# Narrow heads as row tiles of TensorE: two heads side by side, operand rows kept by chunk of tokens

## The chip, the cores and the metric

One core of one Trainium2 chip runs the whole program. The time is device microseconds of one execution. The kernel before takes 4517.99 us, the median of three runs (4517.69 to 4519.41).

## The reference, cut to what matters

The program is a stack of residual blocks on 2048 tokens of 128 features. Four of them hold attention with 16 heads of 8 features each; one of the four is causal. Per head it computes

```python
q = (x @ Wq + bq); k = (x @ Wk + bk); v = (x @ Wv + bv)      # 2048 x 128, cut into 16 heads of 8
scores = einsum('bhqd,bhkd->bhqk', rope(q), rope(k)) / sqrt(8)
scores = where(causal, scores, -inf)                          # one of the four
out = einsum('bhqk,bhkd->bhqd', softmax(scores), v)           # heads joined: 2048 x 128
x = x + out @ Wo + bo
```

The kernel treats the 2048 tokens as one sequence. Two of the four attentions stand in gated blocks, where sigmoid scales per head replace the rotation. Everything else (convolution, experts, quantised feed-forward) is not touched by the change.

## The kernel before, in words

The program is a list of stages, each with a part for every engine. An attention is a stage `Prepare`, a stage `Heads` and a projection.

**Prepare.** The tokens are cut into 4 chunks of 512 (`NC` chunks of `CH`). For each chunk TensorE projects to q, k and v, VectorE (and GpSimd for the rotation) transforms them, TensorE turns q and k so that features lie on partitions (L1471), and ScalarE and VectorE split each float32 value into three bfloat16 parts, high, middle and low (L1499 to L1527). SyncE then stores the parts to DRAM (`parts_dram`, L1537, two DMAs of 384 KB a chunk) and gathers them back as operand rows (`gather_rows`, L1299 to L1308). A product of two numbers in three parts each has 9 terms, so a head of 8 features becomes 72 rows (`KR` = `TERMS` x `HD`), plus 3 rows for the maximum (`KM` = 75). One operand tile holds one head at partitions 0 to 74, four heads behind one another, for one group of four heads (`QP`, `KP`); two groups have room at a time. Prepare gathers group 0, chunk by chunk: 6 DMAs of 96 KB a chunk. The groups 1 to 3 are gathered by SyncE within `Heads`, 6 DMAs of 384 KB each, while earlier groups are worked on. The source of each gather has its three repeated or successive parts as the outermost dimension (L1307).

**Heads.** The work is cut into 16 units, a unit being one group of 4 heads and one chunk of 512 queries. `HeadsPlan` writes out one order of steps that every engine follows. For a unit there are two passes. The first finds the maximum of each query's scores: TensorE multiplies 128 queries with 512 keys into one bank (L1732; in the causal attention the diagonal block gets a mask added by an identity product, L1735), and VectorE reduces the bank to its maximum (L1817). There are 64 such maxima a unit (16 to 64 in the causal attention); three banks take turns, so maximum n+3 waits for the reduction of maximum n. VectorE then joins and splits the maxima (L1824 to L1835), TensorE turns them (L1740), VectorE copies them out (L1841), and SyncE sends them through DRAM (L1706, L1708) into the three extra rows of the query operand. The second pass: for each tile j of 128 keys and each of the 4 heads TensorE multiplies keys with the 512 queries (L1752, mask L1755), ScalarE takes the exponential of two banks at once (L1793; L1796 and L1797 where the widths differ), and TensorE multiplies with the values (L1767), four heads as column tiles of 32 columns of the array, float32, 8 instructions for one j. The scores take turns in two pairs of banks. After the last j ScalarE copies the result (L1804), TensorE turns it (L1776), and VectorE divides by the sums (L1850, L1852).

In the plan the maxima of the next units are laid between the scores of the current one: a clock ticks once for each pair of score products, and the maxima of a unit are spread so that they end `LEAD` = 8 ticks before its scores begin; the turn of the maxima comes 3 ticks after their last. The values of a batch of two j follow one batch later. For one j the order on TensorE is thus score, maximum, score, maximum, and so on, four of each, and then the 8 value instructions.

Of the kernel before, what the change touches and what calls it, by code (L numbers as in the profile page):

```python
# [23 lines left out]
NG = HEADS // GH  # L24
SPLIT = 3
TERMS = SPLIT * SPLIT
# [14 lines left out]
             wqkv2=3 * P, bqkv2=3 * P, wo2=P, bo2=P, cos2=NT * 16, sin2=NT * 16, iota=E,  # L41
             ka=KD, kab=KD, kc=NK)
LATE = dict(wqkv3=3 * P, bqkv3=3 * P, wo3=P, bo3=P, cos3=NT * 16, sin3=NT * 16,
# [61 lines left out]
class Chip:  # L105


    def __init__(self, ctx, nc, d, out):
# [33 lines left out]
        self.mr = sb("mr", [P, 2, 16])  # L142
        self.nmb = sb("nmb", [P, 2, 3 * 16], BF16)
# [9 lines left out]
        self.parts_dram = nc.dram_tensor("parts_dram", (2, SPLIT, NG, HD, GH * T), BF16, kind="Internal").ap()  # L153
# [1128 lines left out]
def qkv(c):  # L1282
    return c.arena[:, 16384:16384 + NT * 384].rearrange("p (i n) -> p i n", i=NT)


def rotated(c):
    return c.arena[:, 4096:4096 + NT * 256].rearrange("p (i n) -> p i n", i=NT)


def packed(c):  # L1290

    both = c.arena[:, 0:16384].bitcast(BF16).rearrange("p (w s h t) -> p w s h t", w=2, s=2, h=GH)
    return both[:, 0], both[:, 1]


GATHERS = 2 * SPLIT


def gather_rows(e, c, g, t0, n, marks):  # L1299
    QP, KP = packed(c)  # L1300
    slot = g % 2
    for a in range(SPLIT):
        rows = slice(SPLIT * HD * a, SPLIT * HD * (a + 1))
        for dst, which, first, step in ((QP, 0, a, 0), (KP, 1, 0, P * T)):
            src = bass.AP(tensor=c.parts_dram.tensor,
                          offset=(which * SPLIT + first) * P * T + g * HD * GH * T + t0,
                          ap=[[step, SPLIT], [GH * T, HD], [T, GH], [1, n]])  # L1307
            e.dma_start(dst[rows, slot, :, t0:t0 + n], src).then_inc(marks.sem, 16)  # L1308


class Rope:


    def __init__(self, chip, cos, sin):
        self.c, self.cos, self.sin = chip, cos, sin
        self.src = rotated(chip)
        self.v = chip.sig.claim("rope_vector", 3 * NC)
        self.g = chip.sig.claim("rope_gpsimd", 3 * NC)
        half = GH * HD // 2
        self.x = qkv(chip)[:, :, 0:2 * P].rearrange("p i (g a n) -> p i g a n", a=2, n=half)  # L1320
        self.r = self.src[:, :, :].rearrange("p i (g a n) -> p i g a n", a=2, n=half)
        self.tmp = [[chip.arena[:, at:at + CH].rearrange("p (i g n) -> p i g n", i=TPC, g=2 * NG)
                     for at in range(12288 + 2048 * b, 12288 + 2048 * (b + 1), CH)] for b in range(2)]

    def factors(self, k):
        half = GH * HD // 2
        span, shape = slice(TPC * k, TPC * k + TPC), (P, TPC, 2 * NG, half)
        cs = self.cos.rearrange("p (i n) -> p i n", i=NT)[:, span, :].unsqueeze(2).broadcast_to(shape)
        sn = self.sin.rearrange("p (i n) -> p i n", i=NT)[:, span, :].unsqueeze(2).broadcast_to(shape)
        return span, self.x[:, span, :, 0, :], self.x[:, span, :, 1, :], cs, sn, self.tmp[k % 2]  # L1330

    def vector(self, e, k, made):
        span, x1, x2, cs, sn, tmp = self.factors(k)
# [8 lines left out]
        e.tensor_tensor(self.r[:, span, :, 0, :], tmp[0], tmp[1], ALU.subtract).then_inc(self.v.sem, 1)  # L1342

    def gpsimd(self, e, k, made):
        span, x1, x2, cs, sn, tmp = self.factors(k)
# [8 lines left out]
        e.tensor_tensor(self.r[:, span, :, 1, :], tmp[2], tmp[3], ALU.add).then_inc(self.g.sem, 1)  # L1354
# [9 lines left out]
class Temper:  # L1364


    def __init__(self, chip, scale):
        self.c, self.scale = chip, scale
        self.src = qkv(chip)
        self.prod = chip.arena[:, 4096:4096 + NT * P].rearrange("p (i n) -> p i n", i=NT)  # L1370
        self.zs = chip.arena[:, 6144:6144 + NT * HEADS].rearrange("p (i n) -> p i n", i=NT)
        self.v = chip.sig.claim("temper_vector", 7 * NC)
        self.s = chip.sig.claim("temper_sigmoid", NC)

    def z(self, k):
        return self.zs[:, TPC * k:TPC * k + TPC, :].rearrange("p i n -> p (i n)")

    def vector(self, e, k, made):
        span, z, v = slice(TPC * k, TPC * k + TPC), self.z(k), self.v
        e.wait_ge(*made)  # L1380
        e.tensor_tensor(self.prod[:, span, :], self.src[:, span, 0:P], bc(self.scale, TPC), ALU.mult).then_inc(v.sem, 1)
        e.wait_ge(*v[7 * k])
        e.tensor_reduce(z, self.prod[:, span, :].rearrange("p i (g d h) -> p (i g) h d", g=NG, h=GH), AX,
                        ALU.add).then_inc(v.sem, 1)
        e.wait_ge(*self.s[k])
        e.tensor_scalar(z, z, 2.0, None, ALU.mult).then_inc(v.sem, 1)
        e.wait_ge(*v[7 * k + 2])
        z4 = z.rearrange("p (i g h) -> p i g h", g=NG, h=GH)
        for g in range(NG):
            q4 = self.src[:, span, 32 * g:32 * g + 32].rearrange("p i (d h) -> p i d h", h=GH)  # L1390
            e.tensor_tensor(q4, q4, z4[:, :, g, :].unsqueeze(2).broadcast_to((P, TPC, HD, GH)),
                            ALU.mult).then_inc(v.sem, 1)

    def scalar(self, e, k):
        z = self.z(k)
        e.wait_ge(*self.v[7 * k + 1])
# [5 lines left out]
    def ready(self, e, k):  # L1402
        e.wait_ge(*self.v[7 * k + 6])


class Prepare(Stage):


    def __init__(self, chip, before, weights, bias, transform):
# [4 lines left out]
        self.ones = sig.claim("rows_of_ones", 2)  # L1414
# [10 lines left out]
        self.gathered = sig.dma("gather0", GATHERS * NC)  # L1425
        self.rem = chip.arena[:, 22528:22528 + 2 * CH].rearrange("p (a n) -> p a n", a=2)
# [999 lines left out]
```

## Time and profile before

| what | us |
|---|---|
| median of three runs | 4517.99 |
| the profiled execution, its own time | 4526.3 |
| span of that execution | 4524.5 |
| TensorE busy in it | 3962.3 |
| VectorE busy | 3194.4 |
| ScalarE busy | 2199.4 |

Two spans of time matter in the pages behind this table: an instruction's own duration, and the distance from its start to the start of the next one on its engine, which is shorter, since instructions overlap. In the profile the clock granted to TensorE is 1.00 at full speed (2.4 GHz) and 0.50 at half (1.2 GHz).

### The profile page before, as it was taken

The page shows a single profiled execution, that of the slowest core. Times are in us where ns is not written, and L with a number is a line of the kernel's source. Part 1 is how long each engine was busy: PE and PEld are TensorE (multiplying, and loading weights), DVE is VectorE, ACT ScalarE, POOL GpSimd, SP SyncE. Part 2 cuts the span into 40 slices and gives each one's busy share as a digit, 9 for nine tenths or more (in the row PEclk, how much of TensorE's full clock was granted, in tenths as well). Part 3 has the DMA queues.
Part 4 walks back from the last instruction along what each step waited for, and adds up shares of the span by engine and source line. Part 5 has one row for each costly group of instructions (what it writes and reads, how often), then busy time and mean ns, then how long its engine had stood idle before and what let it go on. Part 6 is the DMA issues. An engine that isn't in the chain of part 4 may idle for free.

```text
span 4524.5 us, 59451 instructions
## 1 busy us (share of the span) xinstructions
PE 3962.3 (88%) x22108; PEld 1619.8 (36%) x22108; DVE 3194.4 (71%) x6776; ACT 2199.4 (49%) x2694; POOL 97.5 (2%) x59
## 2 busy tenths in 40 slices
PE   5989797599999984999999986399894899999986
PEld 3756655122222232222222363133232232222253
DVE  5256255688888835888888548486774888888546
ACT  2222321166666651466666721156473266666721
POOL 0000000200000001000000001100001000000000
PEclk8889898599999995799999988599897699999988
DMA  0011500100000002000000000100001000000000
GB/s 23 4 43 25 116 1 6 70 1 22 2 22 2 2 6 77 12 2 22 22 2 1 20 1 0 70 2 23 22 2 47 24 2 22 11 13 2 1 19 10
DMA packets 37282, 87.42 MB, mean 19 GB/s; under 512 B 7080, under 2 KB 31432, under 8 KB 32200
## 3 DMA queue, kind: packets, MB, share of 16 engines
q1 hardware_dynamic: 36856, 82.09, 5.7%
q8 instruction: 182, 2.98, 0.3%
q10 hardware_dynamic: 144, 1.53, 0.1%
q14 instruction: 100, 0.82, 0.1%
HBM read 68.91 MB, written 14.70 MB: 18 GB/s over the span
## 4 chain that ended last, share of the span: by engine, by line
PE 75%; DVE 16%; DMA 3%; ACT 2%; SPq 2%; issue 2%; POOL 0%; ACTq 0%; DVEq 0%
PE ps L1767 18%; PE ps L1752 18%; PE ps L1732 15%; DVE pm L1817 8%; PE ps L945 3%; PE ps L948 3%; PE ps L2058 3%; PE ps L1024 3%; PE ps L2034 3%; SPq L1308 2%; DMA m_dram<-mt 1%; PE ps L1458 1%; DVE XN L289 1%; PE ps L1208 1%; PE ps L744 1%
## 5 line engine op out<-in xcount | busy, mean ns | idle before, releaser
L1817 DVE TENSOR_REDUCE pm<-ps 128x1 f32<-128x512 f32 (+2 forms) x3712 | 2258.9, 669 | 453.6 <-PE ps L1732 413.8
L1793 ACT ACTIVATE arena<-ps 128x1024 f32<-128x1024 f32 x1728 | 1684.8, 1022 | 791.5 <-PE ps L1752 788.1
L1732 PE MATMUL ps<-arena 72*128 72x512 bf16 (+2 forms) x3712 | 1453.5, 398 | 154.3 <-DMA arena<-parts_dram 127.6
L1752 PE MATMUL ps<-arena 75*128 75x512 bf16 (+1 forms) x3712 | 1385.7, 382 | 57.1 <-DMA arena<-m_dram 52.1
L1767 PE MATMUL ps<-arena,VA 128*16 128x512 f32 (+2 forms) x7424 | 965.7, 592 | 0.0
L1752 PEld LDWEIGHTS ps<-arena 75*128 75x128 bf16 x3712 | 357.1, 98 | 1098.6 <-issue 771.5
L1732 PEld LDWEIGHTS ps<-arena 72*128 72x128 bf16 x3712 | 368.6, 100 | 672.9 <-DVE pm L1817 338.0
L1767 PEld LDWEIGHTS ps<-arena,VA 128*16 128x16 f32 x7424 | 122.9, 94 | 310.8 <-issue 299.8
L976 DVE TENSOR_TENSOR arena<-EV,ps 128x512 f32<-128x512 f32 x128 | 87.8, 686 | 125.4 <-PE ps L948 120.8
L964 ACT ACTIVATE EV<-ps 128x512 f32<-128x512 f32 x128 | 76.2, 597 | 203.5 <-PE ps L945 203.5
L945 PE MATMUL ps<-XNT,arena 128*128 128x512 f32 x304 | 160.9, 612 | 2.3 <-DVE arena L1251 1.5
L948 PE MATMUL ps<-XNT,arena 128*128 128x512 f32 x304 | 158.4, 603 | 0.0
L315 PE MATMUL ps<-IDF,XN 128*128 128x128 f32 x176 | 51.2, 446 | 108.5 <-DVE XN L289 107.7
L2058 PE MATMUL ps<-arena,EV 128*128 128x512 f32 x256 | 124.1, 629 | 15.5 <-ACT EV L2246 15.5
L1850 DVE RECIPROCAL rd<-ps 128x16 f32<-128x16 f32 x64 | 15.9, 248 | 144.9 <-PE ps L1776 144.8
L1024 PEld LDWEIGHTS ps<-arena 128*128 128x128 f32 x1024 | 115.3, 192 | 2.9 <-issue 2.9
L1024 PE MATMUL ps<-arena 128*128 128x128 f32 x1024 | 115.3, 275 | 0.0
L1793 ACT ACT_TABLE_LOAD x3 | 3.8, 1283 | 225.8 <-PE ps L1752 225.8
L1078 DVE SCALAR_TENSOR_TENSOR X<-ps,prob,X 128x128 f32<-128x128 f32 x256 | 89.7, 351 | 29.1 <-PE ps L1024 22.1
L1796 ACT ACTIVATE arena<-ps 128x512 f32<-128x512 f32 (+1 forms) x128 | 63.0, 492 | 93.9 <-PE ps L1755 93.5
L1458 PE MATMUL ps<-early,XNT 128*128 128x384 f32 x128 | 66.2, 658 | 48.2 <-DVE arena L1487 26.4
L948 PEld LDWEIGHTS ps<-XNT,arena 128*128 128x128 f32 x304 | 59.2, 195 | 75.8 <-issue 74.8
(263 smaller groups left out, 2795.6 us busy)
## 6 DMA issues: line engine op xcount, KB each, us to landing
arena<-parts_dram SPq DMA_DIRECT2D x72, 384.0 KB
parts_dram<-parts SPq DMA_DIRECT2D x32, 384.0 KB, 3.4
arena<-k_dram SPq DMA_DIRECT2D x20, 528.0 KB, 11.2
arena<-parts_dram SPq DMA_DIRECT2D x96, 96.0 KB
parts<-k_dram SPq DMA_DIRECT2D x8, 528.0 KB, 6.4
arena<-in_w SPq DMA_DIRECT2D x4, 1024.0 KB, 6.2
VA<-k_dram SPq DMA_DIRECT2D x4, 528.0 KB, 7.4
arena<-in_w12T SPq DMA_DIRECT2D x1, 2048.0 KB, 13.2
```

Source lines behind the costliest of these rows:

```text
L945: e.matmul(c.bank(b), self.first(j), rhs, start=True, stop=True).then_inc(self.gate.sem, 1)
L948: e.matmul(c.bank(2 + b), self.second(j), rhs, start=True, stop=True).then_inc(self.up.sem, 1)
L1024: ins = e.matmul(c.bank(4 + g % 4)[:, q * P:(q + 1) * P], self.HT[(k - 1) % 2][:, 2 * ex + s, tt * P:(tt + 1) * P], w3[:, 2 * ex + s, :], ...
L1308: e.dma_start(dst[rows, slot, :, t0:t0 + n], src).then_inc(marks.sem, 16)
L1458: e.matmul(c.bank(2 + i % 2)[:, 0:3 * P], c.XNT[:, i * P:(i + 1) * P], self.weights, start=True, stop=True).then_inc(self.projected.sem, 1)
L1732: ins = e.matmul(bank[:, 0:w], QP[0:KR, g % 2, hh, i * P:(i + 1) * P], KP[0:KR, g % 2, hh, kc * CH:kc * CH + w], start=True, stop=not diag)
L1752: ins = e.matmul(bank[:, off:CH], KP[0:KM, g % 2, hh, j * P:(j + 1) * P], QP[0:KM, g % 2, hh, q * CH + off:(q + 1) * CH], start=True, stop ...
L1767: ins = e.matmul(c.bank(4)[32 * hh:32 * hh + VW, off:CH], c.VA[:, j, GH * g + hh, :], self.PB[:, n % self.PBS, jj, off:CH], start=j == 0, ...
L1793: e.activation(self.PB[:, pb, :, :], c.bank(2 * k, 2).rearrange("p (a t) -> p a t", a=2), ACT.Exp, scale=self.scale).then_inc(self.exped.s ...
L1817: e.tensor_reduce(c.pm[:, u % 2, hh * TPC + qt, kc:kc + 1], self.slot_bank(slot)[:, 0:w], AX, ALU.max).then_inc(self.emptied.sem, 1)
L2034: ins = e.matmul(c.bank(2 + h)[:, 0:H1], self.masks[k % 2][:, ex, at:at + P], self.w1[:, ex * H1:(ex + 1) * H1], start=False, stop=ex == E ...
L2058: ins = e.matmul(c.bank(2 + 2 * k + half), self.HTt[k][:, s * P:(s + 1) * P], self.w2[:, s, half * CH:(half + 1) * CH], start=s == 0, stop ...
```

## The change

Two heads become two row tiles of the array. The three least of the nine terms are dropped (six remain, named by `Q_PARTS` and `K_PARTS`), so a head has 48 rows and 51 with its maximum; an even head stands at partitions 0 to 50 and an odd one at 64 to 114. Products of the two heads of a pair go to different row tiles and different banks.

- **Rows by chunk.** `parts_dram` and the operands are laid out by chunk of tokens, with all 8 pairs of heads in each, so all groups are gathered in Prepare: 12 DMAs a chunk, 4 of each of three shapes (3, 2 and 1 terms outermost; 192, 128 and 64 KB). `Heads` gathers nothing and waits once, at its start, for all of them. q, k and v of a chunk are kept for two chunks only.
- **Rows of ones** come by two DMAs instead of a GpSimd memset.
- **Heads.** A maximum is one product of a 48-row tile into one bank as before, odd head first, then even; the two scores of a pair are issued back to back into two banks, and one exponential takes both. In the causal attention both halves of a pair have equal widths, so the exponential stays one instruction. The values of one j are one group of 8 instructions behind the next j's scores.
- **The maxima.** VectorE only joins them; five GpSimd instructions split them; ScalarE copies out the turned rows; two DMAs (one for each row tile) write them into the operand. `LEAD` is 9, and the turn comes 4 ticks after the last maximum.
- **Order.** For one j: a pair of scores, 2 maxima, a pair of scores, 2 maxima, the values of the j before.

```diff
-TERMS = SPLIT * SPLIT
+Q_PARTS = (0, 0, 0, 1, 1, 2)
+K_PARTS = (0, 1, 2, 0, 1, 0)
+TERMS = len(Q_PARTS)
...
-GATHERS = 2 * SPLIT
+GATHERS = 12
...
+def gather_rows(e, c, k, marks):
+    for w, rows in enumerate(packed(c)):
+        for par in range(2):
+            for term, part, step in ((0, 0, w), (3, 1 - w, w), (5, 2 * (1 - w), 0)):
+                n_terms = {0: 3, 3: 2, 5: 1}[term]
+                src = bass.AP(tensor=c.parts_dram.tensor,
+                              offset=((k * 2 + w) * SPLIT + part) * P * CH + par * (P // 2) * CH,
+                              ap=[[step * P * CH, n_terms], [PAIRS * CH, HD], [1, PAIRS * CH]])
+                first = par * (P // 2) + term * HD
+                e.dma_start(rows[first:first + n_terms * HD, k, :, :], src).then_inc(marks.sem, 16)
...
-    LEAD = 8
+    LEAD = 9
...
-        steps = [(u, hh, qt, kc) for hh in range(GH) for qt in range(TPC)
-                 for kc in range(k + 1 if self.causal else NC)]
+        steps = [(u, pp, qt, kc, par) for pp in range(2) for qt in range(TPC)
+                 for kc in range(k + 1 if self.causal else NC) for par in (1, 0)]
...
+                    self.score_pair(u, j, pp)
+                    for _ in range(n):
+                        self.run(pending.pop(0))
+                    self.tick()
+                waiting.append((u, j, first, j == n_keys - 1))
+                if len(waiting) > 1:
+                    self.values(*waiting.pop(0))
...
     def gpsimd(self, e):
+        for u in range(len(self.plan.units)):
+            k = u % 2
+            e.wait_ge(*self.top[u])
...
+            e.tensor_scalar(c.neg[:, k, :], c.mx[:, k, :], -1.0, None, ALU.mult).then_inc(s.sem, 1)
+            e.tensor_copy(c.nmb[:, k, 0:16], c.neg[:, k, :]).then_inc(s.sem, 1)
+            e.tensor_tensor(c.mr[:, k, :], c.neg[:, k, :], c.nmb[:, k, 0:16], ALU.subtract).then_inc(s.sem, 1)
+            e.tensor_copy(c.nmb[:, k, 16:32], c.mr[:, k, :]).then_inc(s.sem, 1)
+            e.tensor_tensor(c.nmb[:, k, 32:48], c.mr[:, k, :], c.nmb[:, k, 16:32], ALU.subtract).then_inc(s.sem, 1)
...
     def tensor(self, e):
+        e.wait_ge(*self.gathered)
...
+                rows = slice(64 * par, 64 * par + KR)
+                ins = e.matmul(bank[:, 0:w], QR[rows, q, 2 * g + pp, qt * P:(qt + 1) * P],
+                               KT[rows, kc, 2 * g + pp, 0:w], start=True, stop=not diag)
...
+                for par in range(2):
+                    rows = slice(64 * par, 64 * par + KM)
+                    ins = e.matmul(c.bank((t + par) % 4)[:, off:CH], KT[rows, j // TPC, 2 * g + pp, j % TPC * P:(j % TPC + 1) * P],
+                                   QR[rows, q, 2 * g + pp, off:CH], start=True, stop=not diag)
```

## Rows read from the trace of the kernel before

**Rows 1.** The page's header, and chain shares by engine (its part 4).
```profile
span 4524.5 us, 59451 instructions
PE 75%; DVE 16%; DMA 3%; ACT 2%; SPq 2%; issue 2%; POOL 0%; ACTq 0%; DVEq 0%
```
**Rows 2.** Windows: stretch, length, busy time and instructions per engine, clock, DMA share, GB/s.
```profile
770.00:855.80 85.80, 28.27 (x81) 16.90 (x80) 44.45 (x94) 16.02 (x29) 33.35 (x19) 0.64 0.19 65
900.40:1600.00 699.60, 693.84 (x3862) 207.04 (x3863) 617.13 (x1078) 471.61 (x490) 0.00 (x0) 0.99 0.02 8
990.80:1037.27 46.47, 46.13 (x262) 13.85 (x261) 41.13 (x73) 31.73 (x33) 0.00 (x0) 1.00 0.01 2
```
**Rows 3.** Timeline of one j in a plain attention: start, length, engine, line.
```profile
1000.65 0.38 PE L1752 MATMUL ps<-arena 75*128 75x512 bf16 x1
...
1000.87 0.38 PE L1732 MATMUL ps<-arena 72*128 72x512 bf16 x1
...
1001.18 1.05 PE L1767 MATMUL ps<-arena,VA 128*16 128x512 f32 x8
1002.16 0.39 PE L1752 MATMUL ps<-arena 75*128 75x512 bf16 x1
...
1002.39 0.38 PE L1732 MATMUL ps<-arena 72*128 72x512 bf16 x1
...
1002.81 2.48 DVE L1817 TENSOR_REDUCE pm<-ps 128x1 f32<-128x512 f32 x4 [0.35 <-PE ps L1732]
...
1003.02 1.94 ACT L1793 ACTIVATE arena<-ps 128x1024 f32<-128x1024 f32 x2 [0.89 <-PE ps L1752]
...
1003.48 0.38 PE L1752 MATMUL ps<-arena 75*128 75x512 bf16 x1
```
**Rows 4.** Groups by form: busy us, mean ns, idle before.
```profile
L1817 DVE TENSOR_REDUCE pm<-ps 128x1 f32<-128x512 f32 x3520 | 2195.9, 682 | 415.6 <-PE ps L1732 413.8 <-PE ps L1735 1.1
L1735 PE MATMUL ps<-MQB,IDB 128*128 128x128 bf16 x256 | 60.4, 237 | 0.0
L1446 POOL TENSOR_TENSOR parts<-arena,parts 128x512 bf16<-128x512 f32 x16 | 18.5, 1154 | 107.4 <-ACT parts L1527 107.4
L2419 POOL MEMSET const-bfloat16-1.0<- 128x1 bf16 x1 | 0.1, 113 | 0.0
```
**Rows 5.** Timeline: a maximum waits for its bank.
```profile
1551.90 2.47 DVE L1817 TENSOR_REDUCE pm<-ps 128x1 f32<-128x512 f32 x4
...
1552.63 0.10 PEld L1732 LDWEIGHTS ps<-arena 72*128 72x128 bf16 x1 [0.83 <-DVE pm L1817]
```
**Rows 6.** The chain at the start of the first Heads: start, length, what.
```profile
847.78 7.98 DMA arena<-parts_dram
...
856.52 38.36 DVE pm L1817 x64
...
896.66 1.39 DMA m_dram<-mt
898.06 2.28 DMA arena<-m_dram
```
**Rows 7.** Timeline of SyncE's queue at the end of the first Prepare.
```profile
815.38 4.64 SPq L1308 DMA_DIRECT2D arena<-parts_dram  x6
822.62 2.86 SPq L1537 DMA_DIRECT2D parts_dram<-parts  x2
825.58 5.33 SPq L1308 DMA_DIRECT2D arena<-parts_dram  x6
830.96 2.22 SPq L1537 DMA_DIRECT2D parts_dram<-parts  x2
833.29 21.04 SPq L1308 DMA_DIRECT2D arena<-parts_dram  x18
```
**Rows 8.** Windows in which only gathers move (columns as in rows 2).
```profile
848.00:852.00 4.00, 0.00 (x0) 0.00 (x0) 0.00 (x0) 0.00 (x0) 0.00 (x0) 0.50 0.20 72
2892.00:2913.00 21.00, 0.27 (x1) 0.11 (x1) 0.85 (x5) 0.00 (x0) 0.00 (x0) 0.50 0.18 78
```
**Rows 9.** DMA issues by shape: count, KB each, us from issue to landing.
```profile
parts_dram<-parts SPq DMA_DIRECT2D x32, 384.0 KB, 3.4
arena<-in_w SPq DMA_DIRECT2D x4, 1024.0 KB, 6.2
```
**Rows 10.** The two longest pieces of the chain in the causal Heads.
```profile
3173.67 26.55 DMA m_dram<-mt
2893.44 19.37 DMA m_dram<-mt
```
**Rows 11.** Windows: causal Heads; after its second wait; clock beside partly busy TensorE.
```profile
2883.50:3429.00 545.50, 486.06 (x3200) 182.66 (x3200) 380.96 (x780) 293.78 (x467) 0.38 (x1) 0.90 0.04 15
3203.00:3227.00 24.00, 24.00 (x88) 7.95 (x87) 15.39 (x32) 8.79 (x9) 0.00 (x0) 0.50 0.00 1
860.00:870.00 10.00, 10.00 (x18) 1.77 (x17) 10.00 (x18) 0.00 (x0) 0.00 (x0) 0.50 0.19 82
452.30:469.30 17.00, 12.17 (x222) 11.92 (x219) 2.44 (x2) 4.32 (x3) 0.00 (x0) 1.00 0.84 176
```

More of the change, by code:

```diff
@@ L1591, in tick, with keys, score_pair, values @@
                 self.run(item[1])
-    def batches(self, k):
-        n = TPC * (k + 1) if self.causal else NT
-        return [(j, j + 1) for j in range(0, n, 2)]
-    def offsets(self, k, pair):
-        return [max(0, (j - TPC * k) * P) if self.causal else 0 for j in pair]
-    def values(self, items, u, last):
-        for jj in range(2):
-            self.steps.append(("values", u, jj, items, last))
-            yield
+    def keys(self, k):
+        return TPC * (k + 1) if self.causal else NT
+    def score_pair(self, u, j, pp):
+        q = self.units[u][1]
+        off = max(0, (j - TPC * q) * P) if self.causal else 0
+        first = self.tiles
+        self.tiles += 2
+        self.tile_off += [off, off]
+        self.steps.append(("scores", u, j, pp, first))
+        while len(self.exp_of) < self.tiles:
+            t = len(self.exp_of)
+            n = 2
+            self.exp_of += [self.exps] * n
+            self.steps.append(("exp", t, n, self.exps))
+            self.exps += 1
+    def values(self, u, j, first, last):
+        self.steps.append(("values", u, j, first, last))
         if last:
+            self.last_tile[u] = first + 3
             self.steps.append(("empty", u))
-            self.later.append([3, ("out", u)])
+            self.later.append([4, ("out", u)])
     def lay_out(self):
         units = self.units
-        self.steps.append(("gather", 1))
         for step in self.maxima(0):
@@ L1615, in lay_out @@
         for _, k in units:
-            starts.append(starts[-1] + len(self.batches(k)) * GH)
-        pending, reached, queued, total, clock, waiting = [], 0, [], 0, 0, None
+            starts.append(starts[-1] + 2 * self.keys(k))
+        pending, reached, queued, total, clock = [], 0, [], 0, 0
+        waiting = []
         for u, (g, k) in enumerate(units):
-            if u % NC == 0 and 1 <= g < NG - 1:
-                self.steps.append(("gather", g + 1))
-            todo = self.batches(k)
-            for b, pair in enumerate(todo):
-                items = []
-                for hh in range(GH):
+            n_keys = self.keys(k)
+            for j in range(n_keys):
+                first = self.tiles
+                for pp in range(2):
                     while reached < min(u + 2, len(units) - 1):
@@ L1754, in tensor @@
                 if diag:
-                    ins = e.matmul(bank[:, off:off + P], c.IDB[:, :], c.MKB[:, :], start=False, stop=True)
-                if jj == 1:
-                    ins.then_inc(self.scored.sem, 1)
+                    for par in range(2):
+                        ins = e.matmul(c.bank((t + par) % 4)[:, off:off + P], c.IDB[:, :], c.MKB[:, :], start=False,
+                                       stop=True)
+                ins.then_inc(self.scored.sem, 1)
             elif what == "values":
-                _, u, jj, items, last = step
+                _, u, j, first, last = step
@@ L2403, in layout @@
     return {
+        "ones": np.full((1, PAIRS * T // 2), ONE_PAIR, np.float32),
         "x": i["L0_attn_input_data"].reshape(T, P),
```

353 lines of the change are left out of this document (165 added, 188 removed).

## The prediction

> **What bounds the kernel now.** I read the share of each engine in the chain first, then windows by stage, then the timeline of one step within the longest stage, and last what stands in the chain where TensorE is idle. The chain is three quarters TensorE [rows 1]. The three plain attentions make up half of the span: one takes some 740 us in `Heads`, with TensorE busy 99% of it and at the full clock [rows 2]. One unit takes 46.47 us there [rows 2], and one j 2.83 us: seven steps of 0.22 us from product to product, 0.31 from the last product to the values, and 0.98 for the values [rows 3]; 7 x 0.22 + 0.31 + 0.98 = 2.83. Sixteen of these are 45.3 us, and 1.1 us a unit is the rest (turns of maxima and results). VectorE is busy 2.48 of the 2.83 us and waits 0.35 for TensorE; ScalarE works 1.94 [rows 3]. So TensorE is the limit, VectorE not far behind: with a product always ready a reduction starts every 38.36 / 64 = 0.60 us [rows 6], four take 2.40.
>
> Between Prepare and Heads no engine works: from the first gather's issue at 815.4 to its last landing at 855.8 the gathers of the last chunks are waited for [rows 6, 7]. While they alone move, the rate is 72 to 78 GB/s at a DMA share of 0.18 to 0.20, three of sixteen engines [rows 8]; a store of 384 KB takes 3.4 us and a load of 1024 KB 6.2 us, or 165 GB/s [rows 9]. The gathers are slow by their shape, three parts outermost.
>
> **The change part by part.** The sum is made against the profiled execution, 4526.3 us (span 4524.5); that is 8 us above the median of the runs, 4518, to which I apply the differences.
>
> *Scores and maxima, plain attention.* Instructions stay as many. If both heads of a pair run side by side, a pair of scores takes 0.22 us instead of 0.44, its bounds; I take 0.22, since rows of two disjoint halves of the array have no operand in common, and keep 0.44 for a rival. TensorE's own work for a j would fall to about 2.0 us, and something else must be late next. It is not VectorE alone but the banks: three serve four maxima. A maximum whose bank is reduced from time 0 can be issued at 0.73 (1551.90 to 1552.63) [rows 5]: 0.68 of reduction [rows 4] and 0.05 for the signal. For the fourth maximum of a j that is the first one's bank. Behind it on the queue stand the values (0.31, then 0.98), then a pair of scores (0.22), then the next first maximum, whose reduction starts 0.42 after its issue (1002.39 to 1002.81) [rows 3]. The circle is 0.73 + 0.31 + 0.98 + 0.22 + 0.42 = 2.66 us a j, above VectorE's 2.40 and ScalarE's 1.94. So the gain is 0.17 us a j, 2.7 a unit. In the rest of a unit the split of the maxima leaves VectorE, but the join (0.22) and the division (0.56) fall into a circle with no slack, and a slot now waits for ScalarE behind an exponential: I take 0.4 back, so 2.3 a unit.
>
> That holds for 13 units. The first has 3 maxima a tick, 6 a j: VectorE and the banks hold it before and after alike, apart from its first 16 us at half clock, where six maxima and four scores on TensorE cost more than now; I take -4. The last two run out of maxima and are near ScalarE's pace: -2. Heads proper: -4 - 30 - 2 = -36.
>
> *The maxima's way.* At the start of a stage it is bare: 5.5 us from the last maximum to the first score [rows 6]. Four VectorE instructions go (0.85 us with their gaps), five of GpSimd come. The trace has none of their size: 0.11 us for a memset of one column is below, 1.15 for 512 columns above [rows 4]; with 16 columns I take 0.35, 1.8 in all. The second DMA adds its issue, 0.7. So +2 a stage. In steady state the turn is 4 ticks (5.3 us) after the last maximum, so TensorE, which would wait in front of all scores, doesn't: 0.25 + 1.8. From the turn to the scores are 5 ticks, 6.6 us, for 1.5 (ScalarE's queue), 1.4 (to DRAM), 0.7, 2.3 (back) = 5.9: hidden, narrowly. At 1.15 us each the split alone takes 5.8, and each unit would lose some 2 to 3 us: the upper bound.
>
> *Gathers, all of them in front.* Before, a stage gathered 24 x 96 KB = 2.36 MB before its first maximum and the other 7.1 MB behind work. After, it is 4 chunks x 4 x (192 + 128 + 64) KB = 6.29 MB, and TensorE's first maximum waits for all. At 78 GB/s [rows 8] the 3.93 MB more cost 50 us. Nothing hides them: Prepare's own work ends where it did (829), SyncE's 48 issues at 0.77 us (4.64 / 6 [rows 7]) take 37 us and are hidden under the transfers. The last gather waits for the last store, which stands behind gather 1 on its engines; gather 2 was issued before and fills that time. Bounds: spread like a plain load at 165 GB/s, 38 us in all, +7; two- and one-term gathers on only two and one engines (each a third of 78 GB/s, the first of them carrying every gather), 6.29 / 2 MB on each step of 26 GB/s, 121 us, +91. I take +50: half of the bytes have exactly the shape of the row.
>
> The Trainium skill, "DMA: Bandwidth & Descriptors", section "Why a DMA increments its semaphore by 16 and not by 1", says that the slowest dimension of both sides picks the engines: the largest number up to 16 that divides both, the lowest-numbered ones. For a 3-row source that is three engines; by that rule the trace agrees. By it the new shapes use 3, 2 and 8 engines, and the first engine carries 2.2 MB at 26 GB/s, 86 us: 6 us more a stage, a sum higher by some 24.
>
> *Plain attention, sum:* +50 + 2 - 36 = +16, three times +48.
>
> *Causal attention* (545.5 us [rows 11]). +50 and +2 again. But two pieces of its chain go: m_dram writes of 19.37 and 26.55 us that stood behind the gathers of later groups on the same engines; alone one takes 1.39 [rows 6, 10]. That is -43. After the second of them TensorE ran 24 us fully busy at a clock of 0.50 [rows 11]; without the pause I take -8. The pairs save some 59 us of products on TensorE, half on the path. Against it, 256 diagonal maxima [rows 4] and 128 diagonal pairs of scores alternate between 64-row products and a 128-row mask product, 768 changes of shape. The nearest row is the change to and from the value group, 0.31 - 0.22 = 0.09 and 0.98 less 0.85 of columns = 0.13 [rows 3]; none is below. I take 0.06, half on the path, and for both together -5. Sum: +50 + 2 - 43 - 8 - 5 = -4.
>
> The Trainium skill, "TensorEngine Tiling (Array Packing)", section "Key Properties", states that changing the tiling mode drains TensorE. The trace agrees at the values. At 0.11 for every mask change the causal stage would be some 20 us slower than in my sum.
>
> *Prepare.* The same elements in fewer or equal instructions; the memset of GpSimd was hidden; the two-chunk buffers wait for turns that were already waited for: 0.
>
> Total +48 - 4 = +44 us, 4562 on the median.
>
> **The rivals.**
> 1. *The gathers spread* over many engines. For: stores and loads do [rows 9]. Against: the outermost dimension is still 3, 2 or 1. +7 instead of +50, four times: 4390, faster.
> 2. *The circle of the banks is broken* and VectorE's 2.40 to 2.45 is reached, because half-height products deliver sooner or the values are entered without the 0.09 and 0.13. For: VectorE alone holds 0.60. Against: three banks. 0.23 x 16 x 14 x 3 = 155 less: 4407.
> 3. *Row tiles don't overlap.* Circle 2.88 instead of 2.66, above the 2.83 of now: 3.5 us a unit worse than in my sum, 150 for three stages, 35 in the causal one: 4747. No row shows two row tiles together; four column tiles do overlap at the values [rows 3].
> 4. *Gathers narrower:* +91 instead of +50: 4726.
> 5. *The clock stays at half speed.* TensorE is less filled. Through the first unit's maxima, one product in 0.60 us, the granted clock stays at 0.50; but in another stretch, busy 12.2 of 17 us, it stays at 1.00 [rows 11], and at half speed the circle keeps TensorE nearly full, as before its rise now. The circle would be 0.73 + 0.52 + 1.84 + 0.43 + 0.63 = 4.15: some 5600.
>
> **How the numbers follow.** My forecast 0.55, with its own range 4515 to 4610 (shape changes, GpSimd, rate of gathers); rivals 0.12, 0.09, 0.12, 0.08, 0.04. The range 4375 to 4730 leaves out parts of the first, third and last. A measurement can tell about 0.2%, 9 us. Faster: rivals 1 and 2 and 0.08 of my own case (steady gain over 3.5 us a unit), 0.29; within 0.2%: 0.07; slower: 0.64.
>
> **What would show it.** The first maximum of a plain stage some 90 us after the first gather's issue instead of 40, with three engines' rate in between; a j at 2.66 us with VectorE waiting 0.26 of it; two score products starting within 0.05 us; no long m_dram piece in the causal stage. Wrong if gathers move at over 100 GB/s, or if a unit takes under 42 us or over 46.

## The result, and the profile after

The changed kernel takes 4645.6 us (median of 4 runs, 4637 to 4649), the kernel before 4518.7: a ratio of 1.028, 95% interval 1.026 to 1.029. That is 127 us slower, where 44 had been forecast. The profiled execution took 4642.1 us, its span is 115.7 us longer than that of before; the other 11 us are the 8 by which the profiled execution of before lay above its median and the 3.5 by which this one lies below its own. The page of the changed kernel, as in [rows 1]:

```profile
span 4640.2 us, 57712 instructions
PE 60%; DVE 24%; DMA 4%; SPq 4%; issue 4%; ACT 3%; POOL 0%; ACTq 0%; DVEq 0%; POOLq 0%
```
The chain has lost TensorE (75 to 60%) to VectorE and to the gathers with SyncE's queue. Windows of the changed kernel (stretch, length, busy time and instructions of PE, PEld, DVE, ACT, POOL, granted clock, DMA share, GB/s): from the first gather to the first maximum, a part in which only gathers move [rows 8], the first plain Heads, a unit as in [rows 2], and the causal Heads.

```profile
818.62:912.54 93.92, 5.04 (x19) 3.21 (x17) 9.38 (x12) 5.09 (x9) 7.26 (x5) 0.50 0.24 88
855.80:905.00 49.20, 0.00 (x0) 0.00 (x0) 0.48 (x1) 0.00 (x0) 0.00 (x0) 0.50 0.19 70
912.54:1671.52 758.98, 656.98 (x4176) 149.38 (x4176) 644.19 (x1072) 507.35 (x545) 17.33 (x80) 0.95 0.01 1
1099.08:1143.50 44.42, 38.50 (x265) 9.10 (x261) 40.36 (x68) 31.66 (x34) 1.08 (x5) 1.00 0.01 1
2984.97:3519.07 534.10, 501.62 (x3152) 141.31 (x3152) 366.31 (x688) 289.66 (x353) 17.32 (x80) 0.84 0.01 2
```
The same two stages in the kernel before:

```profile
855.89:1643.93 788.04, 773.48 (x4176) 222.22 (x4176) 657.71 (x1152) 509.21 (x529) 0.00 (x0) 0.96 0.03 10
2883.53:3419.55 536.02, 479.73 (x3152) 177.16 (x3152) 373.92 (x768) 292.59 (x465) 0.00 (x0) 0.90 0.04 15
```
The stages cut at the first maximum's product and at the end of the last division give the whole difference of the spans. The forecast's "+2 a stage" for the maxima's way lies behind the first maximum, so it is counted with Heads:

| piece | forecast | measured |
|---|---|---|
| before the first maximum, four stages | +200 | 51.6 + 52.7 + 50.8 + 52.6 = +207.7 |
| Heads, three plain stages | -102 | -29.0 - 29.6 - 35.5 = -94.1 |
| Heads, causal | -54 | -1.9 |
| stages before the first Prepare, and the end | 0 | +5.1 - 0.9 |
| sum | +44 | +115.7 (rounded pieces: 115.9) |

The gathers came within 3 us a stage of the forecast. The causal Heads, which should have gained 54 us, gained 2: that is where the forecast failed. The chain from the last gather to the write of the turned maxima, as in [rows 6]:

```profile
888.84 23.56 DMA arena<-parts_dram
...
913.17 38.36 DVE pm L1864 x64
...
951.97 0.27 POOL neg L1722
...
953.14 0.23 POOL nmb L1730
...
954.25 1.40 DMA m_dram<-mt
```
One j of a plain stage, as in [rows 3]: two products of a pair start in one line of 0.39 us, and VectorE waits 0.21 us of 2.70.

```profile
1102.60 2.48 DVE L1864 TENSOR_REDUCE pm<-ps 128x1 f32<-128x512 f32 x4 [0.21 <-PE ps L1771]
...
1103.35 0.39 PE L1771 MATMUL ps<-arena 48*128 48x512 bf16 x1 [0.35 <-DVE pm L1864]
...
1103.67 1.05 PE L1807 MATMUL ps<-arena,VA 128*16 128x512 f32 x8
...
1104.65 0.39 PE L1792 MATMUL ps<-arena 51*128 51x512 bf16 x2
...
1104.88 0.38 PE L1771 MATMUL ps<-arena 48*128 48x512 bf16 x2
...
1105.30 2.48 DVE L1864 TENSOR_REDUCE pm<-ps 128x1 f32<-128x512 f32 x4 [0.21 <-PE ps L1771]
```
In the causal stage a mask (L1774) of 128 rows stands between maxima of 48 rows:

```profile
3109.71 0.38 PE L1771 MATMUL ps<-arena 48*128 48x512 bf16 x1
3110.02 0.23 PE L1774 MATMUL ps<-MQB,IDB 128*128 128x128 bf16 x1
3110.19 0.39 PE L1771 MATMUL ps<-arena 48*128 48x512 bf16 x1
```
A product of 512 columns normally lets the next start after 0.22 us; here the mask starts after 0.31. The mask has a quarter of the columns, 0.055 us, and the next product starts after 0.17. So each change of shape costs 0.09 to 0.12 us, where I had taken 0.06. For a pair of scores two masks (L1796) follow the pair, one for each bank:

```profile
3112.34 0.39 PE L1792 MATMUL ps<-arena 51*128 51x512 bf16 x2
3112.66 0.28 PE L1796 MATMUL ps<-MKB,IDB 128*128 128x128 bf16 x2
3112.88 0.39 PE L1771 MATMUL ps<-arena 48*128 48x512 bf16 x2
```
Without masks the next products would start 0.22 us behind the pair; they start 0.54 behind it, so the two masks with their changes take 0.32.

### The profile page after: what moved, and what is told of

It is laid out like the page before. It is cut to its first block, busy times and chain, and to the rows that moved or that the text cites. A ratio compares the mean times of both kernels' runs of the same rounds, so it can differ in the third digit from the quotient of the medians.

```text
span 4640.2 us, 57712 instructions
## 1 busy us (share of the span) xinstructions
PE 3634.9 (78%) x22108; PEld 1368.0 (29%) x22108; DVE 3135.8 (68%) x6440; ACT 2190.9 (47%) x2630; POOL 138.7 (3%) x371
## 4 chain that ended last, share of the span: by engine, by line
PE 60%; DVE 24%; DMA 4%; SPq 4%; issue 4%; ACT 3%; POOL 0%; ACTq 0%; DVEq 0%; POOLq 0%
PE ps L1807 18%; DVE pm L1864 17%; PE ps L1771 12%; PE ps L1792 7%; SPq L1321 4%; PE ps L949 3%; PE ps L952 3%; PE ps L2089 3%; PE ps L2065 2%; PE ps L1028 2%; DMA arena<-parts_dram 2%; ACT arena L1830 1%; PE ps L1471 1%; DMA parts_dram<-parts 1%; PE ps L1212 1%
## 5 line engine op out<-in xcount | busy, mean ns | idle before, releaser
L1830 ACT ACTIVATE arena<-ps 128x1024 f32<-128x1024 f32 (+3 forms) x1856 | 1763.9, 1000 | 827.3 <-PE ps L1792 695.0
L1771 PE MATMUL ps<-arena 48*128 48x512 bf16 (+2 forms) x3712 | 1161.8, 403 | 602.2 <-DMA arena<-parts_dram 341.9
L1807 PE MATMUL ps<-arena,VA 128*16 128x512 f32 (+2 forms) x7424 | 982.8, 602 | 2.2 <-ACT arena L1830 1.6
L1792 PE MATMUL ps<-arena 51*128 51x512 bf16 (+1 forms) x3712 | 739.6, 387 | 33.4 <-DMA arena<-m_dram 19.2
L1771 PEld LDWEIGHTS ps<-arena 48*128 48x128 bf16 x3712 | 284.2, 95 | 1246.4 <-DVE pm L1864 866.8
L1792 PEld LDWEIGHTS ps<-arena 51*128 51x128 bf16 x3712 | 185.1, 95 | 937.9 <-ACT arena L1830 670.4
L1843 ACT ACTIVATE mt<-ps 48x128 bf16<-48x128 bf16 x64 | 17.2, 270 | 469.5 <-PE ps L1779 469.5
L1807 PEld LDWEIGHTS ps<-arena,VA 128*16 128x16 f32 x7424 | 121.9, 94 | 206.1 <-ACT arena L1830 157.7
L1722 POOL TENSOR_SCALAR neg<-mx 128x16 f32<-128x16 f32 x64 | 16.2, 252 | 2907.5 <-DVE mx L1873 2907.5
```

Of the source, the lines that this page charges most:

```text
L1771: ins = e.matmul(bank[:, 0:w], QR[rows, q, 2 * g + pp, qt * P:(qt + 1) * P], KT[rows, kc, 2 * g + pp, 0:w], start=True, stop=not diag)
L1792: ins = e.matmul(c.bank((t + par) % 4)[:, off:CH], KT[rows, j // TPC, 2 * g + pp, j % TPC * P:(j % TPC + 1) * P], QR[rows, q, 2 * g + pp, ...
L1807: ins = e.matmul(c.bank(4)[32 * hh:32 * hh + VW, off:CH], c.VA[:, j, GH * g + hh, :], self.PB[:, (first + hh) % self.PBS, off:CH], start=j ...
L1830: e.activation(self.PB[:, s:s + 2, offs[0]:CH], c.bank(t % 4, 2).rearrange("p (a t) -> p a t", a=2)[:, :, offs[0]:CH], ACT.Exp, scale=self ...
```

## The experiments

Theory: in the causal stage the masks cost more by the change, at every clock, and TensorE's lower granted clock takes the rest. Rival: the masks cost before what they cost now, and clock or overlap alone explain the loss. All kernels are variants of the changed one but for e6. Ratios are to the kernel before.

**e1_spread.** Each gather cut into DMAs of one term.
```
-                src = ... ap=[[step * P * CH, n_terms], [PAIRS * CH, HD], [1, PAIRS * CH]])
+                for n in range(n_terms):
+                    src = ... ap=[[PAIRS * CH, HD], [1, PAIRS * CH]])
+                    first = par * (P // 2) + (term + n) * HD
```


> After the change, with each gather of 3 or 2 terms cut into DMAs of one term (8 partitions of 8 KB each, 24 DMAs per chunk instead of 12, same bytes). Theory 1 (the gathers are slow since an outermost dimension of 3 or 2 leaves most DMA engines idle): the stretch from the first gather to the first maximum, 93.9 us in Attention 1 of the changed kernel, falls by 38 to 48 us in each of the four stages, the median to some 4455 to 4495 us. Rival (the bytes or the count of issues on SP's queue bound them): the stretch stays within 10 us, or grows with twice the issues, the median within 4610 to 4690 us. Heads themselves keep their lengths (759, 760, 534, 759 us) but for what the clock does at their start.

4487.1 us, ratio 0.992 (0.991 to 0.994): 158 us less than the changed kernel, and faster than the kernel before. From the first gather to the first maximum's reduction, and while only gathers move:

```profile
815.79:864.06 48.27, 5.65 (x21) 3.31 (x19) 9.36 (x13) 5.09 (x9) 7.25 (x5) 0.50 0.55 171
840.00:850.00 10.00, 0.00 (x0) 0.00 (x0) 0.48 (x1) 0.00 (x0) 0.00 (x0) 0.50 0.52 188
```
94 us have become 48 in the first stage and 54, 52 and 54 in the others (to the first maximum's product), with the same bytes in twice as many DMAs; the share is 0.52 where it was 0.19. Heads kept their lengths within 2 us (757.6, 761.0, 535.0, 758.8). Theory 1 holds: the shape, not the bytes nor the number of issues, made the gathers slow. The Trainium skill, "DMA: Bandwidth & Descriptors", section "Why a DMA increments its semaphore by 16 and not by 1", lets the slowest dimension pick the engines, here 8 of 16 for every gather instead of 3, 2 and 8 by turns: by that rule the trace agrees (0.52 of 16 is 8.3).

**e2_half_masks.** The mask as two products of 64 rows and 64 columns, in the row tile of its own head.
```
-                    ins = e.matmul(bank[:, w - P:w], c.IDB[:, :], c.MQB[:, :], start=False, stop=True)
+                    half = slice(64 * par, 64 * par + 64)
+                    for h in range(2):
+                        at = w - P + 64 * h
+                        ins = e.matmul(bank[:, at:at + 64], c.MH[half, 192 - 64 * h:320 - 64 * h],
+                                       c.IDB[half, half], start=False, stop=h == 1)
```
(and the scores' masks likewise)

> After the change, with the causal mask added in the head's own row tile: two products of 64 rows and 64 columns instead of one of 128 rows and 128 columns, for the maxima and for the scores of attention 3 alone. Theory 1 (each mask product costs some 0.10 us before and 0.10 us behind it for its change of shape, 384 of them): causal Heads fall from 534 us by 30 to 60 us, median 4585 to 4615 us. Theory 2 (causal Heads are slow since TensorE's granted clock stays at half speed there, and the shapes have no share in it): Heads of attention 3 stay within 10 us of 534 and the granted clock there is as before. If the shapes also keep the clock down (their drains leave the array idle), both the length and the stretches at 0.50 shrink together. The other stages stay as they are; the early stages gain some 0.5 us from six small copies.

4598.1 us, ratio 1.017 (1.015 to 1.019), 47 less. The causal Heads fell from 534 to 489 us, the others stayed within 3 us (760.6, 757.5, 756.1): theory 1. A timeline shows the four half masks (L1807) of a pair of scores, which hold TensorE for 0.06 us where the two whole ones took 0.32:

```profile
3106.44 0.22 PE L1807 MATMUL ps<-IDB,MH 64*128 64x64 bf16 x4
3106.50 0.27 PE L1775 MATMUL ps<-arena 48*128 48x256 bf16 x2
```

**e3_maxima_first.**
```
-                    self.score_pair(u, j, pp)
                     for _ in range(n):
                         self.run(pending.pop(0))
+                    self.score_pair(u, j, pp)
```


> After the change, with the two or so maxima of each pair of scores put ahead of that pair in the order that all engines follow, nothing else. Theory 1 (steady Heads run round a circle of TensorE, ScalarE and the four score banks, 2.70 us per j, in which the maxima lie between the exponential's end and the next scores): with the maxima ahead of the wait for the banks, they leave the circle, a unit falls from 44.4 us to 39 to 42 us, plain Heads by 40 to 80 us each, median 4430 to 4540 us. Rival (VectorE's reductions bound it, or TensorE's total work): a unit stays at 44.4 us within 0.7 us, median within 4620 to 4670 us. The other side: the next pair of scores now waits behind maxima whose own banks are not yet reduced, a unit grows to 46 us or more, median above 4670 us.

4601.8 us, ratio 1.017 (1.015 to 1.019), 44 less, but not as theory 1 has it: plain Heads gained 7, 7 and 3 us (3 is what unchanged stages differ from trace to trace), the causal ones 18. One j still took 2.69 us, and now the values waited for ScalarE, behind scores that waited for the previous values:

```profile
1103.77 0.38 PE L1792 MATMUL ps<-arena 51*128 51x512 bf16 x2
...
1104.20 2.19 ACT L1830 ACTIVATE arena<-ps 128x1024 f32<-128x1024 f32 x2 [0.50 <-PE ps L1792]
...
1105.25 1.05 PE L1807 MATMUL ps<-arena,VA 128*16 128x512 f32 x8
1106.23 0.10 PEld L1771 LDWEIGHTS ps<-arena 48*128 48x128 bf16 x2 [0.85 <-DVE pm L1864]
```
**e4_warm.**
```
+        for _ in range(340):
+            e.matmul(c.bank(6), c.IDB[:, :], c.parts[:, 0, 0, 0:CH], start=True, stop=True)
         e.wait_ge(*self.gathered)
```


> After the change, with 340 more products of 128 rows and 512 columns (their result is not used) on TensorE at the start of every Heads stage, in the wait of 84 to 87 us for the gathers. Theory 1 (TensorE starts Heads at half clock and pays for it there): the granted clock is 1.00 at the first maximum, and Heads get shorter by 8 to 20 us in plain stages and 15 to 40 us in the causal one, where it stays at half clock for more than 100 us of the first 250; median 4560 to 4610 us. Rival (the clock of the causal stage follows its own sparse work, whatever it starts with): the causal stage falls back to 0.50 at the same places and Heads 3 gain under 10 us. If half speed at the start is covered by VectorE and ScalarE anyway, the median stays within 4630 to 4660 us.

4765.7 us, ratio 1.053 (1.052 to 1.055). My estimate of the wait's free part was wrong: the fence of the stage releases TensorE at 868.5, so the 75 us of products ended at 943.8, 31 us after the maxima could have begun. What it was made for it still tells. Full array at full clock, then the first maxima of Heads; the last two rows are the same for the causal stage:

```profile
920.00:944.00 24.00, 24.00 (x114) 10.69 (x112) 0.00 (x0) 0.00 (x0) 0.00 (x0) 1.00 0.00 0
947.00:950.00 3.00, 2.79 (x6) 0.50 (x5) 3.00 (x6) 0.00 (x0) 0.00 (x0) 0.54 0.00 0
950.00:953.00 3.00, 3.00 (x6) 0.51 (x5) 3.00 (x6) 0.00 (x0) 0.00 (x0) 0.50 0.02 5
3060.00:3084.00 24.00, 24.00 (x112) 10.77 (x110) 0.00 (x0) 0.00 (x0) 0.00 (x0) 1.00 0.00 1
3084.29:3120.00 35.71, 26.24 (x92) 8.41 (x92) 24.94 (x52) 3.60 (x4) 2.02 (x10) 0.54 0.01 1
```
The clock was down at 0.50 some 6 us after the full-size products, and Heads were 760.2, 760.7, 529.5 and 761.8 us long, as without the warming but for 5 us in the causal stage. The clock did not keep what the stage started with: the rival.

**e5_no_masks and e6_before_no_masks.** The causal masks left out, once of the changed kernel, once of the one before.
```
-               KT[rows, kc, 2 * g + pp, 0:w], start=True, stop=not diag)
-                if diag:
-                    ins = e.matmul(bank[:, w - P:w], c.IDB[:, :], c.MQB[:, :], start=False, stop=True)
+               KT[rows, kc, 2 * g + pp, 0:w], start=True, stop=True)
```
(and the scores' masks likewise; e6 has the same edit on the code of before)

> After the change, with the causal masks left out: no mask product in the maxima or scores of attention 3, so its result is that of a mask that lies outside the diagonal blocks alone. Half masks in the head's own row tile took 45 us off these Heads (533.6 to 488.7 us). Theory 1 (a mask of 128 rows among products of 48 and 51 rows costs by its change of shape, halves cost little): Heads of attention 3 come out at 465 to 485 us, close under the half masks. Rival (each product counts by itself, whatever its shape: a half costs as much per product as a whole): no masks save twice as much again, 440 us or less. If the granted clock falls for the sparse work and not for the masks, stretches at 0.50 stay at the starts of groups of small units, some 100 us of them.

> The kernel before, with the same causal masks left out of attention 3 (same part of the result left out). This tells whether the masks became dearer by the change. Theory 1 (they did: before, one product after the other, a mask of 128 rows costs little more than its own 0.05 us): Heads of attention 3 fall from 535.6 us by 10 to 25 us. Rival (masks cost the kernel before as much as the changed one): they fall by 45 us or more, and then the masks do not explain why the causal stage gained nothing, and the overlap of row tiles, broken at each mask, has to.

One run each: 4599.6 and 4521.1 us. The causal Heads in stretches cut at ends of units: three units, three large ones, four with the small ones between groups, and five (a rest of 3 to 4 us is not shown). "Small" stretches are the first and third, though each has a unit or two of middle size. First the kernel before, then e6, then the changed kernel and e5:

```profile
2883.44:3028.05 144.61, 115.65 (x639) 42.03 (x640) 107.92 (x220) 51.91 (x83) 0.00 (x0) 0.77 0.04 17
3028.05:3141.05 113.00, 112.18 (x793) 41.32 (x791) 79.75 (x166) 81.01 (x115) 0.00 (x0) 1.00 0.06 23
3141.05:3254.16 113.11, 90.04 (x561) 33.83 (x559) 77.97 (x162) 42.87 (x85) 0.00 (x0) 0.82 0.06 22
3254.16:3416.05 161.89, 159.81 (x1141) 58.99 (x1143) 107.44 (x220) 115.66 (x181) 0.00 (x0) 1.00 0.01 2
```
```profile
2882.17:3032.54 150.37, 119.47 (x520) 34.98 (x520) 108.20 (x219) 51.88 (x83) 0.00 (x0) 0.69 0.04 17
3032.54:3141.07 108.53, 106.85 (x681) 33.35 (x680) 79.25 (x166) 80.68 (x115) 0.00 (x0) 1.00 0.06 24
3141.07:3257.57 116.50, 97.62 (x444) 28.91 (x442) 78.56 (x161) 42.96 (x85) 0.00 (x0) 0.69 0.05 22
3257.57:3413.21 155.64, 151.48 (x976) 46.98 (x978) 107.04 (x219) 115.27 (x181) 0.00 (x0) 1.00 0.01 2
```
```profile
2984.99:3132.16 147.17, 134.39 (x640) 35.52 (x640) 106.75 (x199) 50.72 (x62) 4.33 (x20) 0.64 0.01 1
3132.16:3244.14 111.98, 107.44 (x789) 31.14 (x789) 76.97 (x145) 80.74 (x94) 4.33 (x20) 1.00 0.01 2
3244.14:3354.99 110.85, 104.55 (x569) 29.49 (x561) 77.20 (x147) 42.00 (x56) 3.25 (x15) 0.72 0.01 2
3354.99:3514.94 159.95, 152.51 (x1138) 44.04 (x1134) 104.56 (x195) 114.84 (x138) 5.41 (x25) 1.00 0.01 2
```
```profile
2988.88:3123.28 134.40, 113.34 (x522) 26.25 (x522) 104.45 (x200) 49.64 (x62) 4.33 (x20) 0.64 0.01 1
3123.28:3224.29 101.01, 90.29 (x682) 21.19 (x678) 74.83 (x145) 78.43 (x94) 4.33 (x20) 0.98 0.01 2
3224.29:3323.72 99.43, 89.38 (x452) 21.25 (x444) 76.37 (x147) 41.10 (x57) 3.25 (x15) 0.66 0.01 2
3323.72:3470.69 146.97, 130.09 (x972) 31.12 (x972) 102.57 (x194) 111.82 (x138) 5.41 (x25) 0.98 0.01 2
```
Without masks the whole Heads (with the rest) are 485.9 us instead of 534.1 in the changed kernel, and 534.2 instead of 536.0 in the one before. In the second and fourth stretch, at a clock of 0.98 or 1.00, the masks cost 23.9 us after the change and 10.7 before it. Before, 9 of these came back as longer small units (150.4 and 116.5 for 144.6 and 113.1 us), with fewer products but a clock of 0.69 in both instead of 0.77 and 0.82; the m_dram waits there were as long as in [rows 10] together (20.27 and 25.36). The masks did become dearer, and half masks take back 45 of the 48 us. A whole mask does one thing more: it parts two maxima that would overlap. At full clock that costs little, as e10 below shows (0.7 us of 112 with all the other neighbours parted).

The first and third stretch are those of the low clock. In the kernel before they hold the two m_dram waits of [rows 10]; less the 18 and 25 us that those took beyond the 1.4 of a free transfer, they are 126.6 and 88.0 us. The changed kernel has no such wait, yet takes 147.2 and 110.9, at a mean clock of 0.64 and 0.72 (0.77 and 0.82 before). Without masks it takes 134.4 and 99.4 at the same 0.64 and 0.66: 24 us of that was masks, and 19 are left, though the pairs should have made these units shorter too. But this sets stretches without masks against stretches with them. Like with like, e6 less its two waits is 131.5 and 92.5 us, and e5 takes 10 us more than that, at 0.64 and 0.66 against 0.69 and 0.69; the other 9 of the 19 are those by which e6's own small units grew when the clock fell. A clock of 0.50, which is 1.2 of 2.4 GHz, holds for two thirds of these stretches.

**e7_first_and_late.** e3 and the values one j later.
```
-                if len(waiting) > 1:
+                if len(waiting) > 2:
                     self.values(*waiting.pop(0))
```


> After the change, with the maxima ahead of their pair of scores and the values' products one j later still, nothing else. With maxima first alone one j still took 2.69 us, and the values waited there for ScalarE's exponential, which waited for scores that stood behind the previous values (0.22 + 0.43 + 1.02 + 0.99 us). Theory 1 (two circles of the same length: that of the maxima banks, and that of scores, exponential and values): with both opened VectorE's four reductions bound a j at 2.40 to 2.50 us, a unit at 39 to 41 us, plain Heads fall from 758 to 670 to 710 us, median 4370 to 4470 us. Rival (VectorE's wait for a maximum behind the values' 1.05 us stays whatever the order): plain Heads stay at 745 to 755 us, median 4585 to 4615 us.

4606.3 us, ratio 1.020 (1.018 to 1.021), 4.5 us above e3's median; plain Heads 750.2, 751.1 and 747.1, a unit 43.9 us as in e3. The rival: VectorE still waits 0.21 us behind the values in every j.

**e8_all.** The edits of e1, e2 and e7 together.

> After the change, with all four edits: gathers of one term each, half masks, maxima first, values one j later. If they add up: 4645 less 158 (gathers), less 47 (masks), less what maxima first and later values bring in the run beside this one; 4160 to 4270 us if a j takes 2.40 to 2.50 us, 4370 to 4410 us if it stays at 2.69. They need not add in the causal stage, where half masks and later values may take the same waits: up to 20 us more than the sum.

4409.6 us (5 runs), ratio 0.976 (0.974 to 0.978): 236 us less than the changed kernel and 110 less than the one before, so it beats both. The second branch of the expectation, at its upper edge, and near the sum of its parts (158 + 47 + 39 = 244).

**e9_double_maxima.**
```
+                if self.causal and q < 2:
+                    e.matmul(bank[:, 0:w], QR[rows, q, 2 * g + pp, qt * P:(qt + 1) * P],
+                             KT[rows, kc, 2 * g + pp, 0:w], start=True, stop=True)
                 ins = e.matmul(bank[:, 0:w], ...
```


> After the change, with each of the 192 maximum products of attention 3's two smaller kinds of unit (16 or 32 maxima) issued twice into its bank, the second writing the same again. These units lie where the granted clock was 0.50 to 0.77, and TensorE was busy 28 to 30 of 30 us there. Theory 1 (half speed is a state that TensorE stays in for what kind of products it gets there, and at half speed TensorE bounds these units): the clock stays at 0.50 as long or longer, and each doubled product of up to 0.43 us adds to the path; Heads of attention 3 grow from 534 by 40 to 80 us. Rival (the clock falls since too little is issued, and more products lift it): the stretches at 0.50 shrink and Heads stay at 534 us or get up to 20 us shorter. If TensorE did not bound these units at all, the length stays within 10 us with the clock unchanged.

4670.2 us (one run); the causal Heads 557 us, 23 more. That fits neither: the small units grew by 9.5 us (first and third stretch), the large ones, beside which the other doubled products run, by 13.5. The clock of the small units stayed at 0.67 and 0.71 (0.64 and 0.72):

```profile
2987.15:3138.45 151.30, 138.17 (x688) 36.87 (x686) 107.39 (x199) 50.69 (x62) 4.33 (x20) 0.67 0.01 1
3257.01:3373.25 116.24, 110.97 (x608) 31.30 (x604) 77.77 (x148) 41.91 (x56) 3.25 (x15) 0.71 0.01 2
```
More products did not lift it. The small stretches grew by 0.11 us for each of their 87 additional products, where one at half clock takes up to 0.43: TensorE does not bound these units alone.

**e10_no_neighbours.**
```
-        steps = [(u, pp, qt, kc, par) for pp in range(2) for qt in range(TPC)
-                 for kc in range(k + 1 if self.causal else NC) for par in (1, 0)]
+        steps = [(u, pp, qt, kc, par) for par in (1, 0) for pp in range(2) for qt in range(TPC)
+                 for kc in range(k + 1 if self.causal else NC)]
```


> After the change, with the maxima of a unit ordered by parity first, so that maxima next to each other come from the same row tile and can't overlap; the scores' pairs stay. Theory 1 (the overlap of neighbouring maxima has its worth in the circle of the maxima banks: the two that now start 0.22 us apart after the scores start up to 0.22 us apart anyway, since VectorE takes them 0.60 us apart): a j goes from 2.70 to at most 2.75 us, plain Heads within 15 us of 759, median 4630 to 4680 us. Rival (row tiles are what makes the plain stages faster): a j goes back to 2.83 us or more, plain Heads to 780 us or more, median above 4700 us. In the causal stage, where TensorE is busy nearly all the time, up to 20 us more in either case.

4689.1 us, ratio 1.038 (1.036 to 1.040). Plain Heads stayed as they were (758.6, 760.5, 760.4, a unit 44.4): there the overlap of neighbouring maxima is worth nothing, as theory 1 says. The causal Heads grew by 45 us, more than twice what either theory allowed. Second and fourth stretch:

```profile
3142.70:3255.34 112.64, 111.82 (x788) 31.73 (x788) 77.06 (x146) 80.53 (x94) 4.36 (x20) 1.00 0.01 2
3378.15:3563.61 185.46, 183.44 (x1141) 46.63 (x1133) 105.61 (x194) 115.23 (x138) 5.45 (x25) 0.84 0.01 2
```
At full clock the order costs 0.7 us of 112. In the fourth stretch, where the clock is now at 0.50 for a third of the time, it costs 25.5 of 160, with TensorE busy 99%. At half clock TensorE is the limit of these large units. Whether the 25.5 us are the lost overlap or the clock, which fell with it, can't be told apart here.

## Why the prediction was wrong, and where it was right

- *Gathers, +50 a stage: right.* 51.6, 52.7, 50.8 and 52.6, at 70 GB/s and a share of 0.19. *The maxima's way, +2: right,* within Heads: the first scores come 46.1 us after the first maximum where it was 44.5; the GpSimd steps took 0.20 to 0.26 us each (0.35 in the forecast).
- *The circle of the banks, 2.66 us a j: right.* 0.75 + 0.32 + 0.98 + 0.23 + 0.42 = 2.70, a unit 44.42 (46.47 - 2.3 = 44.2 forecast). e3 showed what I had not seen: a second circle (scores, exponential, values) of 2.69 us lies right under the first, and e7 a wait behind the values under both; so VectorE's 2.40 is not reached by these orders.
- *Row tiles overlap: right* (two products of a pair start together). The overlap of neighbouring maxima is worth nothing in plain stages (e10); that of the scores was not taken away in any run.
- *The first unit, -4 a plain stage: wrong.* In Attention 1 it takes 114.7 us from the first maximum to the first division instead of 113.3, of which 1.6 are the maxima's way: nothing gained. The clock rose for good some 60 us after the first maximum before; now it rises after 57 us, but is down once more for 13.6 us:

```profile
983.00:996.60 13.60, 13.60 (x51) 2.20 (x43) 9.01 (x16) 5.12 (x5) 0.00 (x0) 0.50 0.00 0
```
 That is 3.4 us against the -4 + 2; 13 units at 2.05 instead of 2.3 are 3.3 more, and the last two gained 1.8 more than forecast: the 4.9 us by which Attention 1 missed its 34. The second missed by 4.4, the last gained 1.5 more than forecast; since unchanged stages differ by up to 3 us between traces, these small terms are barely above the noise.
- *The causal sum: the step that failed*, by 52 us. "I take 0.06, half on the path, and for both together -5" mis-sized both of its terms, and "without the pause I take -8" had the clock wrong.
  - The changes of shape: 768 x 0.06 / 2 = 23 us were allowed. The masks cost 48 (e5), against 2 before (e6), so 46 by the change. In e6 a lower clock hides part of what the masks cost before; at full clock alone it is 23.9 against 10.7. The only rows for a change of shape had 0.09 and 0.13 [rows 3], and 0.09 to 0.12 is what they cost; half on the path was too little as well: 46 of 768 x 0.10 = 77 us is six tenths. By the Trainium skill, "TensorEngine Tiling (Array Packing)", section "Key Properties", a change of mode drains TensorE; the trace agrees, with those 0.09 to 0.12 us.
  - The pairs, 59 us half on the path, and the clock, -8: together -37.5 forecast. Without masks on both sides (e6, e5) the causal Heads fell by 48.3 us. 42.8 of these are the m_dram waits, and 1.6 go the other way for the maxima's way: some 7 are left. The two stretches at full clock fell from 264.2 to 248.0 us, by 16; the small ones grew by 10. So 30 us of the 37.5 did not come.
  - 59 / 2 - 23 is 6.5, which the forecast set down as 5. 23 + 30 less these 1.5 are the 52, to the rounding.
- *The m_dram waits, -43: gone as forecast;* none over 1.4 us is on the chain of the causal Heads.
- *The clock in the causal stage* went down, not up: its mean is 0.84 where it was 0.90, so half speed holds for a third of the stage instead of a fifth. Rival 5 said that the clock could stay down and gave it 0.04, for all stages or none.
- *Before the first Prepare, 0: +5.1.* Most of it may be chance: in the traces of eight kernels whose code is the same up to there the first gather is issued between 815.6 and 822.1 us (815.4 before). The input of constants has grown from 1496 to 1752 KB, and the first product, which comes behind it, starts 0.5 us later (11.13 instead of 10.63).

What lifts and drops the clock is not settled. It was not the start (e4), not the masks (e5 has 0.64 and 0.66), and doubled products did not lift it (e9). That a lower clock goes with longer causal Heads is seen across the variants that have whole masks: 516 us at a mean of 0.87 (e3), 529 at 0.85 (e4), 534 at 0.84 (changed kernel), 579 at 0.76 (e10). But e3 and e10 changed the order too, and e9 says that the small units do not hang on TensorE alone. So how the 30 us that pairs and clock owed divide between clock, order and other waits is open.

## What to carry to other kernels

When a product is shrunk to part of the array, look at what full-size products stand between the small ones, and price each change from a row that has one; or shrink those too, as the half masks do. In these runs a gather's outermost dimension set how many DMA engines moved it (share 0.18 to 0.20 with 3 outermost [rows 8], 0.52 with 8): one term per DMA moved the same bytes in little more than half the time, which turned this change from 2.8% slower to 0.8% faster. And before a circle of waits is opened, work out the next one: here it was shorter by 0.01 us.

## What the runs showed of the hardware

- After 75 us of products with 128 rows back to back (clock 1.00) the granted clock was 0.54 in a window that began 3.2 us after the last of them and 0.50 in the next, with TensorE busy 93 to 100% on products of 48 rows one at a time (e4).
- Behind a pair of scores, four products of 64 rows and 64 columns in two row tiles took 0.06 us together (e2), where two of 128 rows and 128 columns took 0.32 with their changes of shape. Between maxima of 48 rows one of the latter cost 0.26 (0.09 and 0.17).
- Gathers of 8 partitions of 8 KB moved 188 GB/s at a DMA share of 0.52 (e1), the changed kernel's mix of 3, 2 and 1 terms 70 GB/s at 0.19.
